# Scaling the scattered sums of images 0 to 2 on ScalarE, one 128-column block at a time, in place of VectorE

## What is computed

```
x_flat = groupnorm(x)                              # per image: 1024 points of 128 channels
emb  = x_flat @ dist_w.T                           # 32 values a point
adj  = (the 24 nearest points of each point, and itself)    # 1024 x 1024 of zeros and ones
X_lin = x_flat @ fc_w.T + fc_b
Dv = adj.sum(axis=2);  De = adj.sum(axis=1)
S  = (adj / De) @ adj.T / Dv
out = S @ X_lin + x_flat
y = silu(batchnorm(out));  result = x + y
```

## Time and profile before

| | |
|---|---|
| three runs | 178.42 us median (178.11, 178.42, 182.41) |
| the profiled execution | 178.34 us |
| its span, first to last instruction | 176.5 us |
| mean granted TensorE clock in it | 0.966 of 2.4 GHz |

### The profile page before, as it was taken

How to read it: one execution, slowest core, us unless ns; L and a number is a source line. 1 busy time by engine, 2 the same in 40 slices (tenths; PEclk the granted TensorE clock), 3 DMA queues, 4 the chain that set the end, 5 groups by cost and what they waited for, 6 DMA issues and landing times.

```text
span 176.5 us, 4076 instructions
## 1 busy us (share of the span) xinstructions
PE 153.5 (87%) x1231; PEld 99.6 (56%) x1231; DVE 143.9 (81%) x860; ACT 119.0 (67%) x199; POOL 105.9 (60%) x160
## 2 busy tenths in 40 slices
PE   7799999899989995999999969999999998899000
PEld 2334522556466653676666748667877877879000
DVE  0678999979989870999798989889889985497682
ACT  1267879998787983946578896939663775490590
POOL 1000647879984763598995488998629995371000
PEclk9999999999999999699999999999999999999955
DMA  5821002151937923477155279471659399893057
GB/s 189 270 92 2 2 4 45 16 98 25 124 57 125 94 31 59 97 148 120 24 100 101 20 32 208 79 133 35 121 82 44 57 183 64 174 325 161 0 196 279
DMA packets 45418, 17.72 MB, mean 100 GB/s; under 512 B 41928, under 2 KB 42568, under 8 KB 45392
## 3 DMA queue, kind: packets, MB, share of 16 engines
q1 hardware_dynamic: 44528, 17.03, 50.9%
q10 hardware_dynamic: 864, 0.40, 0.9%
HBM read 6.11 MB, written 2.13 MB: 47 GB/s over the span
## 4 chain that ended last, share of the span: by engine, by line
DVE 70%; issue 8%; PE 8%; ACT 4%; DVEq 3%; another core or an unknown queue 3%; DMA 2%; POOL 1%; ACTq 0%; POOLq 0%
DVE cand L965 34%; DVE cwork L977 10%; DVE top L974 8%; DVE thr L981 4%; DVE t L1042 2%; PE pt L527 2%; DMA x_sb<-x 2%; DVE prod L1061 2%; DVE xn L1146 2%; DVEq L996 2%; DVE gn_stats L932 1%; ACT key L697 1%; DVE least L991 1%; ACT xn L783 1%
## 5 line engine op out<-in xcount | busy, mean ns | idle before, releaser
L965 DVE MAX8 cand<-key 128x8 f32<-128x64 f32 x512 | 79.5, 211 | 0.3
L494 PE MATMUL pt<-xp,H 128*128 128x128 bf16 (+1 forms) x768 | 50.5, 223 | 2.1 <-issue 1.3
L494 PEld LDWEIGHTS pt<-xp,H 128*128 128x128 bf16 x768 | 45.5, 99 | 11.3 <-issue 7.6
L697 ACT ACTIVATE key<-pg 128x512 f32<-128x512 f32 x64 | 34.6, 592 | 20.9 <-PE pg L468 17.7
L468 PE MATMUL pg<-right,left 64*128 64x512 f32 x128 | 40.7, 642 | 4.7 <-issue 2.4
L864 POOL TENSOR_SCALAR H<-sign 128x1024 bf16<-128x1024 bf16 x32 | 33.4, 1044 | 16.1 <-ACT sign L705 16.1
L705 ACT ACTIVATE sign<-key,thr 128x1024 bf16<-128x1024 f32 x32 | 36.8, 1150 | 7.9 <-DVE thr L981 7.8
L468 PEld LDWEIGHTS pg<-right,left 64*128 64x128 f32 x128 | 12.6, 184 | 17.4 <-issue 9.7
L827 POOL CAST x_wide<-HT 128x1024 fp32r<-128x1024 bf16 x12 | 12.2, 1040 | 4.3 <-PE po L527 4.3
L974 DVE MAX8 top<-cand 128x8 f32<-128x128 f32 x32 | 9.0, 280 | 5.8 <-issue 5.8
L547 PE MATMUL pt<-filler 128*128 128x512 bf16 x42 | 12.4, 417 | 1.3 <-POOL filler L788 1.3
(11 more groups left out here) (93 smaller groups left out, 208.0 us busy)
## 6 DMA issues: line engine op xcount, KB each, us to landing
x_sb<-x SPq DMA_DIRECT2D x1, 2048.0 KB, 7.9
out<-xn SPq DMA_DIRECT2D x7, 256.0 KB, 2.1
dvb<-inv_rows SPq DMA_DIRECT2D x3, 512.0 KB, 4.8
x_sb<-x SPq DMA_DIRECT2D x1, 1024.0 KB, 6.0
left<-left SPq DMA_DIRECT2D x6, 128.0 KB, 2.5
x_sb<-x SPq DMA_DIRECT2D x1, 512.0 KB, 3.6
HT<-H SPq DMA_TRANSPOSE x32, 3.3
x_sb<-x ACTq DMA_DIRECT2D x1, 256.0 KB, 3.2
```

The costliest lines, as they stand in the source:

```text
L494: mm = pe.matmul(pt[:, j // T_BLOCKS, at:at + wide], lhs, x_cols(b, t, q, wide), start=(t == 0 and j % T_BLOCKS == 0 and q == 0), stop=(t ...
L697: act.activation(key[:, k % KEYS, cols], pg[:, h, :], ACT.Copy).then_inc(s["drained"], 1)
L965: ins = dve.max(cand[:, k % 2, c, :], key[:, k % KEYS, c * CHUNK:(c + 1) * CHUNK])
```

## The change

For images 0 to 2, VectorE still clamps the degrees and takes the reciprocals, and raises a new semaphore `rde_made` at that point; its four multiplications are gone. ScalarE multiplies in a new function `t_scale`, called just before `t_high(b-1)`: eight ACTIVATE instructions of 128 columns, each from PSUM, each with its own [128,1] column of `rde` as the scale. It raises `t_scaled` after the same blocks as before. The last image keeps VectorE's way. VectorE waits in addition for `t_scaled` of the image before, so as not to overwrite `rde` early. The waits of TensorE, GpSimd and `t_high` on `t_scaled` are unchanged.

```diff
+            def t_scale(b):
+
+                act.wait_ge(s["rde_made"], b + 1)
+                if b > 0:
+                    act.wait_ge(s["t_lo"], 2 * b)
+                at = t_blocks(b)
+                for first, end in zip(at, at[1:]):
+                    for j in range(first, end):
+                        col = j % T_BLOCKS * (C + 1)
+                        ins = act.activation(t32[:, j * C:(j + 1) * C], pt[:, j // T_BLOCKS, col:col + C], ACT.Copy,
+                                             scale=rde[:, j:j + 1])
+                    ins.then_inc(s["t_scaled"], 1)
+
             def t_high(b):
...
                     if b > 0 and t == SCALE_STEP[b] + 1:
+                        t_scale(b - 1)
                         t_high(b - 1)
...
             def scale_t(b):
                 dve.wait_ge(s["h_used"], TILES * (b + 1))
                 if b > 0:
+
+                    dve.wait_ge(s["t_scaled"], 2 * b)
                     dve.wait_ge(s["t_lo"], 2 * b)
...
                 link(ins)
+                if b < B - 1:
+                    dve.reciprocal(rde[:, :], rde[:, :]).then_inc(s["rde_made"], 1)
+                    return
                 link(dve.reciprocal(rde[:, :], rde[:, :]))
```

More of the change, by code:

```diff
@@ L207, in build @@
                  "x_lo limited signed lowered flagged flag_read clipped noise_made settled h_used t_scaled t_hi "
-                 "t_lo rdv_ready rdv_out dvb_in spread dvb_made o_ready o_used y_ready step slow_step stats_done bn_sd "
+                 "t_lo rde_made rdv_ready rdv_out dvb_in spread dvb_made o_ready o_used y_ready step slow_step stats_done bn_sd "
                  "bn_affine silu_done summed filler_set x_back").split()
```

## The result

| | before | changed |
|---|---|---|
| median | 180.41 us (178.11, 178.42, 182.41, 182.47) | 185.06 us (184.4 to 185.23, 4 runs) |
| profiled execution | 178.34 us | 184.4 us |
| its span | 176.5 us | 182.5 us |
| mean granted TensorE clock | 0.966 | 0.934 |

The four runs of the kernel before fall into two groups, 178.1 to 178.4 us and 182.4 to 182.5, so the changed kernel is set against the lower group, to which the profiled execution belongs: the ratio is 1.037, 95% interval 1.033 to 1.042. Between the two profiled executions it is 6.1 us slower, where 0.7 was forecast and the range ended at 182.6.

The account below looks back on a forecast made before the run. TensorE and VectorE were taken to bound it side by side; TensorE's delays of 1.0, 1.6 and 2.2 us at the three scalings, less tail room, left 0.6 to 0.7: 179.1 us, range 176.2 to 182.6.

Parts of the forecast that it names:

- Price of one scaling on ScalarE: At each moved scaling, eight ACTIVATEs of 351 ns, 0.25 us apart, take 2.1 us (bounds 1.4 and 2.8); VectorE took 1.34.
- TensorE waits directly for it, and the delay stays: First scaling: TensorE's next scatter starts 1.8 us later, and with no gap up to 97 us its remaining delay stays.
- I take 0.8 as given back: First scaling: starting later, TensorE loses less to the low clock ending at 75.7 us; 0.8 returns, leaving 1.0 us delay.
- the rival with the falling clock: TensorE's clock falls again behind new idle time at the first two scalings: 180.8 us (one stretch), 182.5 (two); chance 0.28.
- I have no cause for them and give them no part: The 4.49 us before the first scaling, ascribed to an unknown queue, stay as they are and add nothing.
- The flag of pair 10 ends VectorE's gain: Before this flag read VectorE waits about 3.6 us, ending 1.0 us later than before instead of 2.7 earlier.
- The tail gives back 1.6: After the third scaling, 1.0 us of TensorE room and a 0.61 us wait for VectorE absorb delay, leaving 0.6 to 0.7.
- Sign and size without the two accidents: Whole kernel: the change makes it slower, the profiled execution going from 178.34 to 179.0 us.
- VectorE the bound after all: TensorE's delays are absorbed and VectorE's 4.0 us gained: 174.4 us, or halfway 175.7 to 177; chance 0.17.

Follow-up runs that it names:

- e12: The changed kernel with 1/Dv written to DRAM as 128 rows of 32 bytes in place of 1024 single elements: 180.04 us.
- e4: The changed kernel with idle TensorE matmuls at the head of steps 13 and 21 and ahead of the flag in them: 180.95 us.
- e5: The kernel before with 11 idle TensorE matmuls at the head of step 13: 179.38 us.
- e11: The kernel before with 1/Dv written to DRAM as 128 rows of 32 bytes in place of 1024 single elements: 178.13 us.
- e6: The changed kernel without the transfers of 1/Dv to DRAM and back for images 0 to 2, output not the reference's: 178.97 us.
- e7: The kernel before without the transfers of 1/Dv to DRAM and back for images 0 to 2, output not the reference's: 176.50 us.
- e10: The changed kernel with idle TensorE matmuls in steps 13 and 21 and VectorE's removed multiplications put back as dummies: 182.75 us.
- e8: The changed kernel with ScalarE's scaling put ahead of the mark of the tile before instead of behind it: 183.93 us.
- e13: The changed kernel with idle TensorE matmuls in steps 13 and 21 and ScalarE's scaling ahead of the mark of the tile before: 183.95 us.
- e2: The kernel before with only image 1 scaled on ScalarE, images 0 and 2 left on VectorE: 180.56 us.

## Why the prediction was wrong

- **Price of one scaling on ScalarE: right.** 2.1 us was forecast for the eight; at the first two scalings ScalarE's rows read

```profile
72.64 2.17 ACT L717 ACTIVATE t<-pt,rde 128x128 f32<-128x128 f32 x8
...
108.49 2.18 ACT L717 ACTIVATE t<-pt,rde 128x128 f32<-128x128 f32 x8
```

  One takes 392 ns rather than 351; its neighbours overlap it by more. The estimate from ScalarE: Activation LUTs, of the Trainium skill ("What ACT_TABLE_LOAD costs"), 386 ns, lies nearer for one instruction, and 2.4 us for eight lies further off.
- **TensorE waits directly for it, and the delay stays: right.** The scatter of tile 8 was forecast 1.8 us late; it is 2.14, of which 0.2 was there before the scaling. From there to 100 us the delay did not shrink.
- **"I take 0.8 as given back": wrong.** The low stretch did not end at 75.7 us but at 80; the gather that began at 77.41 took 2.48 us. The delay was 3.1, not 1.0. It was the rival with the falling clock that came, at both scalings. I had it, gave it 0.28, and worked out each stretch as one of 3.4 us: 182.5 with two. There were three more than before, one at the first scaling and two at the second.
- **"I have no cause for them and give them no part": the step that failed.** The 4.49 us in the chain were an event with a cause, the write of 1/Dv in single elements, and the second write has the same effect on a handover that falls into the time before some 10 us behind its issue (behind the third no trace shows a wait). At the second scaling it held the handover to ScalarE, which cost TensorE 1.8 us (fill of tile 27 at 107.04, 4.9 us late, where the fill before was 3.1 late) and made the idle time behind which the clock fell. No rival contained it. Without the write's single elements the changed kernel takes 180.04 (e12), inside the forecast's range.
- **The flag of pair 10 ends VectorE's gain: right in place.** A wait of 3.6 us was forecast; it is 4.40, and 3.40 in e4, which has no second standstill.
- **The tail gives back 1.6: right.** It gives back 1.8.
- **Sign and size without the two accidents:** 0.7 us was forecast. It is 1.6 us with idle matmuls (e4 against e5, low clock in e5 alone), 1.9 with the write in rows (e12 against e11, low clock in both), 2.5 without the transfers (e6 against e7, low clock in the trace of e6 alone). The sign was right and the size too small by a factor of two to four. All lie in the forecast's own range for ScalarE's price, at its upper side (2.8 us).
- **VectorE the bound after all:** this rival did not come, but VectorE's relief is not worth nothing either: 1.8 of 4.0 us (e10).

## What to carry to other kernels

An idle stretch in a trace with no releaser is a term of the sum and not scenery. Find out what was issued up to 10 us ahead of it before moving anything near, and look whether the same thing is issued again later: a small delay elsewhere can push another handover into its next copy. When a step is moved to the engine that has time, ask first who waits for its result. Here there was one set of sums in PSUM, so 0.8 us more of scaling, and the queue ahead of it, became a wait of the fullest engine. And a clock that fell once behind idle time can fall for longer (6.8 us here for the 3.4 seen), so price such a rival by more than one stretch a place; then ask whether the time would be lost anyway in a wait that ends at a fixed moment, as in e8 and e13.

## What the runs showed of the hardware

- A write of 1024 single 4-byte elements from SBUF to DRAM held up semaphore increments of TensorE until 9.1 to 10.8 us after its issue, and in one trace one of VectorE to itself (e13, 1.45 us). At the first place of the kernel before it kept ScalarE idle for 2.80 us, with TensorE's fill started at 67.40 and taken up at 70.30. The same data in 128 rows of 32 bytes did not (e11, e12). TensorE goes on meanwhile, and not every increment is late (one of VectorE to TensorE passed within 0.1 us at 104.65).
- TensorE's granted clock fell to the lower level behind gaps of 2.0 to 3.2 us, stayed there for 3.4 or 6.8 us, and did not fall when idle matmuls filled the gaps. Two gaps of that size brought no fall: 2.01 us at 104.2 in e6, where the same gap brought one in e2 and e12, and 2.23 us at 151.7 in e10. TensorE: Matmul & The Clock Gate, of the Trainium skill (Part 1), says that idleness halves the clock and activity frees it, which these runs bear out.
- A VectorE product of 512 columns, PSUM by SBUF, with the SBUF operand read at a stride of 32 bytes took 1.09 us where the contiguous one took 0.69.
